# Attention with an even stream of score maxima: three rounds of eight exponentials, masked scores kept in the bank, FP4 weights expanded in place

## The reference, cut to what matters

```python
scores = jnp.einsum('bsnh,btnh->bnst', k, q) / math.sqrt(HEAD_SIZE)   # b=2, n=16 heads, 1024 x 1024
scores = jnp.triu(scores) + -10000.0 * jnp.tril(ones, k=-1)
attn = jax.nn.softmax(scores, axis=2)
out = jnp.einsum('bnkq,bknh->bqnh', attn, v)
...
nib = w[:, :, None] >> shifts & jnp.uint32(15)
vals = _FP4_LUT[nib.astype(jnp.int32)].reshape(out_f, in_p * 8)
return vals * s_full
```

## Time and profile before

| | us |
|---|---|
| median of 3 runs | 2069.95 (2061.15 to 2071.49) |
| the profiled execution | 2079.13 |
| its span, first to last instruction | 2077.3 |
| attention, first maximum unit to last value unit | 171.2 to about 567.4 |
| mean granted TensorE clock, whole span | 0.94 |

### The profile page before, as it was taken

One profiled execution on the slowest core, in us unless ns is written; L12 is line 12 of the kernel. 1 busy time (PEld: TensorE's weight loads), 2 busy tenths in 40 slices (PEclk: granted clock), 3 DMA queues, 4 the chain that ended last, 5 costly groups with the idle time before them and its releaser, 6 DMA issues. The chain is left out here.

```text
span 2077.3 us, 24075 instructions
## 1 busy us (share of the span) xinstructions
PE 1822.1 (88%) x7553; PEld 1284.7 (62%) x7553; DVE 993.3 (48%) x2218; ACT 609.8 (29%) x1184; POOL 482.3 (23%) x790
## 2 busy tenths in 40 slices
PE   6996999998898999999689999978878788878886
PEld 5884444444476877878567677755556555655554
DVE  5435767676551232322485677783333333333332
ACT  3121555554521122121232422202323222222222
POOL 2003333335610000000242411112222222222222
PEclk9996999999999999999889999988999899999998
DMA  6235567665309000000200111138787788778784
GB/s 238 105 140 135 151 167 190 175 169 156 106 18 334 0 1 1 1 0 1 99 1 1 62 44 44 41 116 271 249 283 246 251 264 261 263 257 267 233 288 128
DMA packets 129323, 298.91 MB, mean 144 GB/s; under 512 B 23952, under 2 KB 34704, under 8 KB 128976
## 3 DMA queue, kind: packets, MB, share of 16 engines
q1 hardware_dynamic: 114896, 262.11, 36.9%
q0 software_dynamic: 14336, 35.66, 8.5%
HBM read 232.66 MB, written 60.46 MB: 141 GB/s over the span
## 5 line engine op out<-in xcount | busy, mean ns | idle before, releaser
L799 ACT ACTIVATE probs<-bank 128x512 f32<-128x512 f32 (+3 forms) x384 | 169.1, 497 | 196.4 <-PE bank L740 190.9
L1748 POOL DMA_INDIRECT out_x<-e_y,row_out x64 | 100.9, 1576 | 488.4 <-ACT e_y L1806 469.8
L1784 PE MATMUL bank<-w_gate,xgt 128*128 128x352 f32 x512 | 211.9, 570 | 0.0
L1852 DVE TENSOR_TENSOR e_hidden<-e_silu,bank 128x352 f32<-128x352 f32 x64 | 33.4, 521 | 273.3 <-issue 222.4
L1784 PE MATMUL bank<-w_up,xgt 128*128 128x352 f32 x512 | 162.4, 460 | 0.0
L724 PE MATMUL bank<-k_stack,q_stack 96*128 96x512 f32 (+3 forms) x384 | 142.8, 400 | 20.2 <-DMA k_stack<-qk_parts 10.4
L740 PE MATMUL bank<-q_stack,k_stack 98*128 98x512 f32 (+3 forms) x384 | 142.4, 399 | 19.7 <-DMA q_stack<-neg_max_t 12.0
L1784 PEld LDWEIGHTS bank<-w_gate,xgt 128*128 128x128 f32 x512 | 119.2, 245 | 62.6 <-issue 38.2
L222 PE MATMUL bank<-ln_xt_hi,gu_hi 128*128 128x512 f32 x352 | 141.3, 401 | 14.4 <-DMA gu_lo<-fp_out 9.7
L1764 PE MATMUL bank<-ident,xg 128*128 128x128 f32 x256 | 51.2, 331 | 116.5 <-DMA xg<-expert_rows,row_in 115.6
L754 PE MATMUL bank<-probs,v_ones 128*64 128x512 f32 (+3 forms) x768 | 148.4, 524 | 0.0
(11 more groups left out here) (233 smaller groups left out, 3800.9 us busy)
## 6 DMA issues: line engine op xcount, KB each, us to landing
w_gate<-in_w_gate SPq DMA_DIRECT2D x64, 704.0 KB, 5.6
w_up<-in_w_up SPq DMA_DIRECT2D x64, 704.0 KB, 7.6
w_down<-in_w_down SPq DMA_DIRECT2D x64, 512.0 KB, 8.0
q_stack<-qk_parts SPq DMA_DIRECT2D x96, 128.0 KB, 3.1
k_stack<-qk_parts SPq DMA_DIRECT2D x96, 128.0 KB, 3.5
w_down<-in_w_down SPq DMA_DIRECT2D x64, 192.0 KB, 8.7
fp_words<-in_fp_words SPq DMA_DIRECT2D x32, 264.0 KB, 3.2
fp_out<-fp_hi SPq DMA_DIRECT2D x32, 264.0 KB, 2.2
```

The lines of the kernel that those rows point to most:

```text
L799: act.activation(probs[u % PROBS][:, 0:cols], m.bank[EXPB[u % 3]][:, 0:cols], ACT.Exp, scale=scale).then_inc(exp_ready, 1)
L1748: pool.indirect_dma_start(out=a["out"][:, :], out_offset=bass.IndirectOffsetOnAxis(ap=row_out[u][:, :], axis=0), in_=y[u % 2][:, :], in_of ...
L1784: last = pe.matmul(m.bank[bank[u % 2]][:, 0:F], xt[u % 2][:, k, :], w[u][:, k, :], start=(k == 0), stop=(k == KT - 1))
```

## The change

1. The maxima become one stream over the pairs. Before pair 0 come its 24 units, the turn, and the first `LEAD = 8` units of pair 1. In pair p there are 24 slots, one behind each exponential unit, and VectorE follows the same order: slots 0 to 15 hold units 8 to 23 of pair p+1, slots 16 and 17 the units 0 and 1 of pair p+2, slot 18 the turn of pair p+1, the others the units 2 to 7 of pair p+2. The turn takes its place in the ring of three banks, and one semaphore (`max_bank_read`) counts all reads of it. The join comes behind slot 15.
2. Three rounds of eight exponential units instead of four of six, so the value units come in batches of eight. `copy_out(p, 0)` moves to the third exponential of the last round.
3. VectorE's FP4 work is laid out anew: `vector_bits(2p)` behind slot 2, `vector_lo(2p-1)` behind slot 6, `vector_bits(2p+1)` behind slot 10, `vector_lo(2p)` behind slot 20, the inversion of the sums behind slot 22.
4. The masked scores of L841 are written back to the PSUM bank that they are read from; `wide_mask` is bf16 instead of fp32.
5. FP4 in place: the shifted words overwrite the words; the low part overwrites `fp4_scaled`. So `gpsimd_scale(n)` now waits until slice n-1 has been stored to HBM, not only until its low part is made.

```diff
-        self.hi, self.lo = put("fp4_hi", [P, SLICE], F32R), put("fp4_lo", [P, SLICE], F32)
+        self.hi, self.lo = put("fp4_hi", [P, SLICE], F32R), self.scaled
...
-        dve.tensor_scalar(self.spread[:, :], self.words[n % 2][:, :], self.shift[:, :], 19, ALU.logical_shift_left,
+        dve.tensor_scalar(self.words[n % 2][:, :], self.words[n % 2][:, :], self.shift[:, :], 19, ALU.logical_shift_left,
...
     def gpsimd_scale(self, pool, n):
         pool.wait_ge(self.bits_ready, n + 1)
-        need(pool, self.lo_ready, n)
+        need(pool, self.stored, 32 * n)
...
-    ROUNDS = 4
-    EXP_ROUND, MAX_ROUND = U // ROUNDS, U // (ROUNDS - 1)
+    ROUNDS = 3
+    EXP_ROUND = U // ROUNDS
+    LEAD, TURN_AT = 8, 18
+
+    def maxima_of(p):
+
+        first = [] if p >= 0 else [("unit", 0, n) for n in range(U)] + [("turn", 0)] + [("unit", 1, n) for n in range(LEAD)]
+        for n in range(U if p >= 0 else 0):
+            if n == TURN_AT and p + 1 < PAIRS:
+                first.append(("turn", p + 1))
+            q, i = divmod(U * (p + 1) + n + LEAD, U)
+            if q < PAIRS:
+                first.append(("unit", q, i))
+        return first
...
-                need(pe, max_part_ready, u - 2)
-                bank = m.bank[MAXB[u % 3]]
+                need(pe, max_bank_read, at - 2)
...
+            maxima(maxima_of(-1))
             pe.wait_ge(ones_set, 2 * SLOTS + 4)
...
-                    for n in range(EXP_ROUND):
-                        exp_unit(p, EXP_ROUND * r + n)
-                        while scored_ahead < ahead * (n + 1) // EXP_ROUND:
-                            max_unit(p + 1, MAX_ROUND * r + scored_ahead)
-                            scored_ahead += 1
-                        if r == ROUNDS - 1 and n == 2 and p + 1 < PAIRS:
-                            turn_max(p + 1)
+                    for n in range(EXP_ROUND * r, EXP_ROUND * (r + 1)):
+                        exp_unit(p, n)
+                        maxima(ahead[len(ahead) * n // U:len(ahead) * (n + 1) // U])
...
-                        if n == 2 and r == 3:
+                        if n == 2 and r == 2:
                             copy_out(p, 0)
...
-                    dve.tensor_tensor_reduce(out=masked[u % 4][:, 0:cols], in0=m.bank[MAXB[u % 3]][:, 0:cols], in1=wide_mask[:, CH - cols:],
+                    dve.tensor_tensor_reduce(out=bank[:, 0:cols], in0=bank[:, 0:cols], in1=wide_mask[:, CH - cols:],
...
+                for n in range(U):
+                    maxima(ahead[len(ahead) * n // U:len(ahead) * (n + 1) // U])
+                    if n == 2:
+                        dq.vector_bits(dve, 2 * p)
+                    if n == 6 and p >= 1:
+                        dq.vector_lo(dve, 2 * p - 1)
+                    if n == 10:
+                        dq.vector_bits(dve, 2 * p + 1)
+                    if n == 20:
+                        dq.vector_lo(dve, 2 * p)
+                    if n == 22 and p >= 1:
+                        invert(p - 1)
```

More of the change, by code:

```diff
@@ L471, in vector_bits @@
         need(dve, self.scaled_ready, n)
-        dve.tensor_scalar(self.bits[:, :], self.spread[:, :], 0x8E00, 0, ALU.bitwise_and,
+        dve.tensor_scalar(self.bits[:, :], self.words[n % 2][:, :], 0x8E00, 0, ALU.bitwise_and,
                           ALU.bitwise_or).then_inc(self.bits_ready, 1)
@@ L517, in attention_phase @@
     U = 2 * N
-    ROUNDS = 4
-    EXP_ROUND, MAX_ROUND = U // ROUNDS, U // (ROUNDS - 1)
+    ROUNDS = 3
[10 more added lines that the diff above has]
+        return first
+    place = {entry: i for i, entry in enumerate(entry for p in range(-1, PAIRS) for entry in maxima_of(p))}
     FIRST_DONE = 2 * TPC
@@ L530, in attention_phase @@
     probs = [arena.put(f"probs{i}", [P, CH], F32) for i in range(PROBS)]
-    wide_mask = arena.put("wide_mask", [P, CH], F32)
-    masked = [arena.put(f"masked_scores{i}", [P, CH], BF16) for i in range(4)]
+    wide_mask = arena.put("wide_mask", [P, CH], BF16)
     parts = [arena.put(f"max_parts{i}", [P, 2, 2, QT], F32) for i in range(2)]
@@ L590, in place_max @@
                 slot = p % SLOTS
-                sp.wait_ge(max_copied, p + 1)
+                sp.wait_ge(max_bank_read, place["turn", p] + 1)
                 for j in range(2):
@@ L717, in max_unit, with maxima @@
                 q, half, cols = MAX_UNITS[i]
-                u, slot = U * p + n, p % SLOTS
+                at, slot = place["unit", p, n], p % SLOTS
                 if n == 0:
                     pe.wait_ge(stack_loaded[slot], 192 * (p // SLOTS + 1))
-                    need(pe, max_copied, p)
-                need(pe, max_part_ready, u - 2)
-                bank = m.bank[MAXB[u % 3]]
-                pe.matmul(bank[:, 0:cols], qs[slot][j][0:ROWS, q * P:(q + 1) * P],
+                need(pe, max_bank_read, at - 2)
+                pe.matmul(m.bank[MAXB[at % 3]][:, 0:cols], qs[slot][j][0:ROWS, q * P:(q + 1) * P],
                           ks[slot][j][0:ROWS, half * CH:half * CH + cols], start=True, stop=True).then_inc(max_scored, 1)
             def turn_max(p):
+                at = place["turn", p]
                 pe.wait_ge(neg_ready, p + 1)
-                pe.matmul(m.bank[MAXB[0]][0:4 * QT, 0:P], top[:, :, :, :].rearrange("p j a q -> p (j a q)"), m.ident[:, :],
+                need(pe, max_bank_read, at - 2)
+                pe.matmul(m.bank[MAXB[at % 3]][0:4 * QT, 0:P], top[:, :, :, :].rearrange("p j a q -> p (j a q)"), m.ident[:, :],
                           start=True, stop=True).then_inc(max_turned, 1)
+            def maxima(entries):
+                for kind, *which in entries:
+                    if kind == "unit":
+                        max_unit(*which)
+                    else:
+                        turn_max(*which)
             def exp_unit(p, n):
@@ L862, in copy_max, with maxima @@
                     dve.wait_ge(max_placed[(p - 2) % SLOTS], 64 * ((p - 2) // SLOTS + 1))
-                dve.tensor_copy(top_t[p % 2][:, :], m.bank[MAXB[0]][0:4 * QT, 0:P]).then_inc(max_copied, 1)
+                dve.tensor_copy(top_t[p % 2][:, :], m.bank[MAXB[place["turn", p] % 3]][0:4 * QT, 0:P]).then_inc(max_bank_read, 1)
+            def maxima(entries):
+                for kind, *which in entries:
+                    if kind == "turn":
+                        copy_max(*which)
+                    else:
+                        max_part(*which)
+                        if which[1] == U - 1:
+                            join_max(which[0])
             def invert(p):
@@ L871, in _ @@
             dve.wait_ge(wide_masked, 1)
[L872 to L875 removed]
+            maxima(maxima_of(-1))
             for p in range(PAIRS):
[L877 to L893 removed]
+                ahead = maxima_of(p)
+                for n in range(U):
[10 more added lines that the diff above has]
+                        invert(p - 1)
             def split_attn(t):
```

50 lines of the change are left out of this document (11 added, 39 removed).

## The result

The kernel after the change takes 2144.85 us (median of 4 runs, 2142.85 to 2149.06) against 2070.72 (4 runs, 2061.15 to 2073.24) for the kernel before beside it: ratio 1.037, 95% interval 1.0333 to 1.0406. It is slower, as forecast, and 20 us above the 2125 of the forecast, inside its range. The profiled execution took 2145.69 us, its span is 2144.0.

What follows compares the result with a forecast made beforehand. No engine is full throughout: VectorE paces the score phases and stands still in value batches. 13 x (27.85 - 23.4) = +58, and -3 for other pairs, give 2069.95 + 55 = 2125 us; range 2066 to 2150.

Steps and rivals of the forecast that it cites:

- The stall: At the 11th slot VectorE's second bits instruction waits about 4 us for GpSimd's scaling in each of pairs 1 to 13.
- the loop through SP: Late scaling delays VectorE, PE, batch, turn and SP's placing and next loads: period 25.95 us before the clock term.
- the lost wait for placed maxima: At a pair's head the PE no longer waits for the placing, which takes 3.9 us from issue to first use.
- first load to the end of the scaling: In the pair loop, stack loads to store landing 12.1 us, plus scaling with semaphore 1.3: 13.4 us.
- Case 1: Pair loop as forecast, the wait at the 11th slot closing a loop through SP: 2098 to 2146 us, chance 0.72.
- The clock: After the PE's rest, 1.2 GHz stretches the value batch from 2.3 to 4.2 us: period 25.95 + 1.9 = 27.85 us.
- The even stream: In the attention's pairs, if nothing else waits: 21.9 us a pair against 23.4, a gain of 20 us.
- The third phase: Last score phase of a pair, its low part waiting for ScalarE's high part: 4.0 to 5.0 us, summed as 4.5.
- rival 2: Slice scaled before VectorE reaches the 11th slot, so the even stream wins: 21.9 us a pair, 2047 us; chance 0.12.
- PSUM: Masked maxima written to PSUM: nothing taken; if dear, +9 to +20 us on the forecast, chance 0.08.
- Rivals 2 and 3: At the 11th slot: no wait, 2047 us, 0.12; or odd store lands in 2.7 us and effects cancel, 2069, 0.08.
- Pairs 14 and 15: Pairs without stack loads: pair 14 gains 1 us, pair 15 nothing; with pair 0's 2 us, together -3.

Runs made afterwards that it cites:

- the dummy products: Kernel after, with 20 further matmuls per pair ahead of the PE's wait in pairs 1 to 13: 2153.28 us, ratio 1.0396.
- without FP4: Kernel after, with FP4 arithmetic and its loads left out, stores of zeros kept: 2033.32 us, ratio 0.9837; the kernel before likewise: 2046.94 us, 0.9888.
- both repairs: Kernel after, with an fp4_lo tile of its own and vector_bits(2p+1) moved from slot 10 to behind slot 20: 2096.86 us, ratio 1.0137.
- own tile: Kernel after, with fp4_lo in its own tile, so that the scaling waits for lo_ready and not the store: 2106.49 us, ratio 1.0164.
- the three runs with a repair: Kernel after with vector_bits(2p+1) behind slot 20, with a separate fp4_lo tile, or with the two together: 2098.88, 2106.49 and 2096.86 us.
- late bits: Kernel after, with vector_bits(2p+1) moved from slot 10 to behind slot 20, nothing else: 2098.88 us, ratio 1.0135.
- FP4 in the batches: Kernel after, with FP4 steps moved into the value batches, stores and words requeued, separate fp4_lo tile: 2058.07 us, 0.9948; with one high part later 2048.23, 0.9921.

## Why the prediction was right, and where it was not

**The stall: right.** Place, waiting instruction, what it waits for, the loop through SP and the lost wait for placed maxima all show in the trace, and an `fp4_lo` tile of its own takes the wait for the scaling away. Its terms, in the pair above: first load to the end of the scaling 14.14 against 13.4 (the store landed 12.95 us after the first load; 12.1 was taken); bits and slots 2.80 against 1.85 (at the low clock, which the working had not counted there); batch 3.35 against 4.2 (the PE had 1.6 us of units before it, so less of the low stretch fell on the batch); turn, placing and next load 8.50 against 8.4. Sum 28.79 against 27.85; over pairs 1 to 13 it is 28.45, 8 us more in all than forecast. The wait was said to be about 4 us in every pair that loads stacks; pair 1 has none, and elsewhere a part of it lies ahead, at the words. Case 1's own range, to 2146, holds the time.

**The clock: right in kind, short in reach.** The fall at the stall is there, at 1.2 GHz, and the working put it there. It had no row for a second fall, behind a phase in which the PE never stops long but is thinly used. That one costs 1.6 us in the 3.7 us batch. Here the loop through SP covers it: the next stack loads are issued at 355.97, inside this batch, and don't wait for its end. In the runs without the stall it comes out.
The Trainium skill (TensorE: Matmul & The Clock Gate, "Part 1: The HAM clock gate") has the throttled clock as the default and activity as what releases it. The runs agree: the dummy products hold 1.00 through the stall, and without FP4 pairs 1 to 13 are at the full clock throughout.

**The even stream: the step that failed, hidden by the stall.** The forecast had 21.9 us a pair wherever the stall is away. With both repairs pairs 1 to 13 take 25.04. Term by term:

| | first phase | second | third | batch behind the first | second | third | pair |
|---|---|---|---|---|---|---|---|
| forecast, us | 4.3 | 4.8 | 4.5 | 2.3 | 2.3 | 3.7 | 21.9 |
| both repairs, us | 4.32 | 4.30 | 6.17 | 2.82 | 2.30 | 5.13 | 25.04 |

Two terms were too small. The third phase, "4.0 to 5.0", takes 6.2; of that 1.0 comes with the bits that the repair puts there, for without them it takes 5.2, in the kernel after and with the low part's own tile (the second phase is 0.5 shorter for it). And the batches were priced at the full clock, 8.3 us in all; behind the thinly fed phases they take 10.25. With the own tile alone, where the bits stay in the second phase, the pair is no shorter (25.46): the phases take 4.34, 5.66 and 5.20, the batches again 10.25.

So the two parts of the sum were off in opposite directions: I priced the even stream at -20 us and the stall at 13 x (27.85 - 21.9) = +77; by the medians of the three runs with a repair the stall is worth 38 to 48, and the stream with the FP4 work in its phases costs 27 to 34. That the total came out near is in part luck. A reader who had trusted rival 2 would have repaired the stall and found the kernel still slower.

**PSUM: right.** No row showed it, nothing was taken, and the run with this edit alone gives 1.0017. Under that cover the price is 59 ns for each read of the sum (142 against 83) and in the kernel after 11 to 22 ns for the instruction, 16 x 76 ns = 1.2 us a pair (1.4 in the run with this edit alone).
**Rivals 2 and 3: out.** VectorE did wait for the scaling, in pairs 2 to 13. The odd store lands 6.0 us after its issue (334.16 to 340.13), not 2.7.

**Pairs 14 and 15: the gain came, and a cost with it that the sum had at nothing.** From first weight load to first weight load pair 14 is 0.9 us shorter, where 1 was said. It holds a new wait all the same: with the turn behind the last exponential the PE waits 2.15 us for the negated maxima (until 605.18), as it does for 4.43 us without FP4, and the 3.7 us batch behind takes 5.3. Pair 15, at nothing in the forecast, costs 5.65 us. About half of that is the clock under the last value units, 16 of them in the kernel after and 12 in the one before:

```profile
563.34 4.09 PE L754 MATMUL bank<-probs,v_ones 128*64 128x512 f32 x24
```
```profile
627.10 8.71 PE L774 MATMUL bank<-probs,v_ones 128*64 128x512 f32 x32
```
```profile
628.00:630.00 2.00, 2.00 (x8) 0.71 (x6) 0.00 (x0) 0.00 (x0) 0.00 (x1) 0.50 0.76 271
```

At the full clock the 16 would take 3.6 + 2.3 = 5.9 us. What the other half is stays open.

## What to carry to other kernels

Before work is spread evenly over an engine's stream, list for each piece what it waits for, and place it where its engine is idle *and* that wait is over: here the batches of another engine's work, and not the slots between the maxima. When two buffers are merged, the reader of the second inherits the waits of the first, a DMA's landing included; follow that wait through the in-order queue that issues the DMA, in both directions. And a stretch in which the PE is only thinly fed costs twice, in itself and in the dense stretch behind it, so a forecast needs a line for the clock after each sparse phase and not only after a stop.

## What the runs showed of the hardware

The granted clock falls to 1.2 GHz without a long stop of the PE. With late bits the fall follows a window in which it was busy for 0.70 of 2 us (336 to 338), its longest wait there 1.30 us; with FP4 in the batches it follows one of 1.16 of 2 us (321 to 323). Short VectorE instructions can be held up beside GpSimd: one of 8 columns took 1.98 us instead of 0.17 beside a product of 1024 columns, once in the 16 joins of the run with late bits, and three of 8 and 16 columns took 0.89 to 1.19 us beside the additions of pair 14 without FP4, as the shift of the earlier trace rows did beside the additions. The read of an accumulated sum takes 142 ns when the instruction ahead of it writes to PSUM, and 83 when it writes to SBUF.
